# Embedding weights on ScalarE's DMA queue with the constants behind them, and a value bias that GpSimd sums for one product

## The reference, cut to what matters

```python
h = conv(x, conv_w) + conv_b + pos_table[pos_ids]       # 16x16 patches, no overlap
z = causal_attention(layernorm(h))                      # v = x W_V + b_V
h = h + einsum('bqhm,hmd->bqd', z, W_O) + b_O
h = h + moe(layernorm(h))                               # top 2 of 8 experts
```

## Time and profile before

| | |
|---|---|
| median of 3 runs | 194.37 us (193.43 to 194.73) |
| the profiled execution, whole time | 194.5 us |
| its span in the profile | 192.7 us |
| TensorE busy | 183.2 us, 95% of the span |
| VectorE, ScalarE, GpSimd busy | 123.9, 91.5, 65.3 us |
| TensorE's mean granted clock | 0.991 of full speed |

### The profile page before, as it was taken

One profiled execution on the slowest core, in us unless ns is written; L12 is line 12 of the kernel. 1 busy time (PEld: TensorE's weight loads), 2 busy tenths in 40 slices (PEclk: granted clock), 3 DMA queues, 4 the chain that ended last, 5 costly groups with the idle time before them and its releaser, 6 DMA issues.

```text
span 192.7 us, 4810 instructions
## 1 busy us (share of the span) xinstructions
PE 183.2 (95%) x1883; PEld 170.4 (88%) x1883; DVE 123.9 (64%) x371; ACT 91.5 (47%) x187; POOL 65.3 (34%) x99
## 2 busy tenths in 40 slices
PE   7999999999999999999999699999999999999991
PEld 2798999998898999998989586899999999999991
DVE  0257966876671065999897638788468467396283
ACT  2046530135455603466596445765857647553210
POOL 8632500114004000168568417550452514406000
PEclk9999999999999999999999969999999999999999
DMA  6999978007100000001108330115949579414544
GB/s 187 384 415 418 389 238 330 3 2 241 37 0 16 3 0 5 3 16 42 52 12 234 135 97 12 31 34 141 425 139 328 153 267 321 146 39 108 152 117 125
DMA packets 11642, 27.94 MB, mean 145 GB/s; under 512 B 3309, under 2 KB 6474, under 8 KB 10436
## 3 DMA queue, kind: packets, MB, share of 16 engines
q1 hardware_dynamic: 8868, 24.92, 38.0%
q0 software_dynamic: 2208, 2.21, 4.1%
q10 hardware_dynamic: 544, 0.50, 0.9%
HBM read 24.22 MB, written 5.77 MB: 156 GB/s over the span
## 4 chain that ended last, share of the span: by engine, by line
PE 70%; DMA 11%; DVE 8%; ACT 4%; issue 3%; POOL 1%; SPq 1%; POOLq 1%; DVEq 0%; ACTq 0%
PE ps L380 8%; PE ps L662 7%; PE ps L459 6%; PE ps L490 6%; DMA slots<-row,slot 3%; PE ps L625 3%; PE ps L647 3%; PE ps L644 3%; PE ps L626 3%; PE ps L648 3%; DMA kT<-parts 3%; PE ps L437 3%; DMA xp<-patches 3%; PE ps L466 2%; PE ps L440 2%
## 5 line engine op out<-in xcount | busy, mean ns | idle before, releaser
L1029 POOL DMA_INDIRECT parts<-qT,toke x12 | 17.9, 1490 | 30.6 <-ACT qT L903 28.8
L1265 DVE TENSOR_TENSOR wqkv<-raw,wqkv 128x1024 fp32r<-128x1024 f32 x16 | 19.6, 1222 | 4.1 <-ACT wqkv L826 3.4
L662 PE MATMUL ps<-xp,v 128*123 128x192 f32 x128 | 22.1, 326 | 0.0
L1354 DVE TENSOR_TENSOR v<-v,ps 128x246 f32<-128x246 f32 x32 | 12.4, 407 | 13.6 <-ACT v L891 13.6
L662 PEld LDWEIGHTS ps<-xp,v 128*123 128x123 f32 x128 | 20.6, 186 | 0.0
L490 PE MATMUL ps<-wo,zs 128*112 128x192 f32 x84 | 16.8, 349 | 1.9 <-ACT zs L792 1.9
L784 ACT ACTIVATE prob<-sm 128x588 f32<-128x588 f32 x8 | 5.7, 707 | 27.3 <-DVE sm L1088 27.3
L625 PE MATMUL ps<-zeA,wqkv 128*128 128x246 f32 x64 | 18.1, 291 | 0.3 <-ACT zeA L884 0.3
L997 POOL DMA_INDIRECT slots<-row,slot x14 | 14.7, 1052 | 9.8 <-DVE row L1180 3.4
L644 PE MATMUL ps<-zeA,wqkv 128*128 128x246 f32 x64 | 17.9, 279 | 0.0
L647 PE MATMUL ps<-zeR,wqkv 128*128 128x246 f32 x64 | 17.8, 278 | 0.0
(11 more groups left out here) (189 smaller groups left out, 475.9 us busy)
## 6 DMA issues: line engine op xcount, KB each, us to landing
raw<-w SPq DMA_DIRECT2D x8, 1024.0 KB, 6.8
xp<-w SPq DMA_DIRECT2D x8, 384.0 KB, 3.3
xp<-patches SPq DMA_DIRECT2D x8, 294.0 KB, 5.0
raw<-w_qkv SPq DMA_DIRECT2D x3, 768.0 KB, 6.0
slots<-blank SPq DMA_DIRECT2D x8, 196.0 KB, 4.4
xp<-slots SPq DMA_DIRECT2D x8, 196.0 KB, 4.4
parts<-zeros SPq DMA_DIRECT2D x1, 1176.0 KB, 8.7
convw<-conv_w SPq DMA_DIRECT2D x2, 288.0 KB, 4.4
```

The source lines that it names most:

```text
L662: last = mm(ps[0:EROWS, 6 + r, 0:D], hT[:, j, jt, r * EROWS:(r + 1) * EROWS], w2s[:, j, jt, :], start=(jt == 0), stop=(jt == JT - 1))
L1029: P.indirect_dma_start(parts, bass.IndirectOffsetOnAxis(toke[:, e, r:r + 1], 0), ye[0:EROWS, e % 2, r, :], None, bounds_check=TOPK * N + E ...
L1265: last = V.tensor_tensor(wsp[:, j, 1, half, :], raw13[j][:, half * W13:(half + 1) * W13], wsp[:, j, 0, half, :].bitcast(f32), ALU.subtract)
```

## The change

The first half of `convw` is no longer SP's first DMA but ScalarE's. ScalarE then waits until it has landed and only then issues the constants, `rowwise` now ahead of `columns`. The fillers of TensorE go from 10 to 8. GpSimd clears one more tile (`onesf`, 128x98, all ones) and, behind `norm` of pairs 0 to 5, sums `wo` times the value bias over the six chunks into `bvw` (128x192): one product, then five times a product and an addition. TensorE multiplies `onesf` by `bvw`, one fp32 matmul in the place of six. ScalarE's copy into `bvx` is gone.

```diff
-        bvx = sb("bvx", [128, HP, PT])
+        bvw = sb("bvw", [128, D])
+        bvc = sb("bvc", [128, D])
+        onesf = sb("onesf", [128, PT])
...
-            sp.dma_start(convw[:, 0:CA], conv_w[:, 0:CA]).then_inc(ld_conv[0], 16)
             sp.dma_start(xp[:, 0], patches[0]).then_inc(ld_x[0], 16)
...
-                pe.wait_ge(ld_wo, 16)
-                pe.wait_ge(bvx_ready, 1)
+                pe.wait_ge(bvw_ready, 1)
                 pe.wait_ge(h_ready, PH)
-                for c in range(HP):
-                    mm(ps[0:PT, 7, 0:D], bvx[:, c, :], wo[:, c, :], start=(c == 0), stop=(c == HP - 1))
+                mm(ps[0:PT, 7, 0:D], onesf[:], bvw[:], start=True, stop=True)
...
-            keep_busy(10, 0)
+            keep_busy(8, 0)
...
+            act.dma_start(convw[:, 0:CA], conv_w[:, 0:CA]).then_inc(ld_conv[0], 16)
+            act.wait_ge(ld_conv[0], 16)
+            act.dma_start(rowwise[:], by_row).then_inc(ld_rowwise, 16)
             act.dma_start(columns[:], by_column).then_inc(ld_columns, 16)
-            act.dma_start(rowwise[:], by_row).then_inc(ld_rowwise, 16)
...
-            A(bvx[:], bv[:, :, None].to_broadcast([128, HP, PT]), ACT.Copy).then_inc(bvx_ready, 1)
...
+            P.memset(onesf[:], 1.0)
             P.memset(seen[:], 0.0).then_inc(all_zeroed, 1)
...
+            def value_bias():
+                nonlocal n
+                pool.wait_ge(ld_wo, 16)
+                pool.wait_ge(ld_columns, 16)
+                P.tensor_scalar(bvw[:], wo[:, 0, :], bv[:, 0:1], 0.0, ALU.mult, ALU.add)
+                for c in range(1, HP):
+                    P.tensor_scalar(bvc[:], wo[:, c, :], bv[:, c:c + 1], 0.0, ALU.mult, ALU.add).then_inc(pool_seq, 1)
+                    n += 1
+                    pool.wait_ge(pool_seq, n)
+                    last = P.tensor_tensor(bvw[:], bvw[:], bvc[:], ALU.add)
+                    if c < HP - 1:
+                        last.then_inc(pool_seq, 1)
+                        n += 1
+                        pool.wait_ge(pool_seq, n)
+                last.then_inc(bvw_ready, 1)
...
             for p in range(EARLY):
                 norm(p)
+            value_bias()
```

More of the change, by code:

```diff
@@ L201, in vit_block @@
         h2T_ready, row_ready, bscale_ready = (sem(x) for x in ("h2T_ready", "row_ready", "bscale_ready"))
-        bvx_ready, bo_done, bo_ready = (sem(x) for x in ("bvx_ready", "bo_done", "bo_ready"))
+        bvw_ready, bo_done, bo_ready = (sem(x) for x in ("bvw_ready", "bo_done", "bo_ready"))
         both_ready, gap_ready, ratio_ready = (sem(x) for x in ("both_ready", "gap_ready", "ratio_ready"))
```

## The result

The changed kernel is slower: a median of 196.11 us (17 runs, 194.5 to 197.2 but for one disturbed execution) against 194.73 for the kernel before on the same chip, a ratio of 1.0089 with a 95% interval of 1.0056 to 1.0122. That is 1.1 to 2.4 us more. The forecast was 192.7 us, 1.7 us less. A second measurement on another chip gave 1.0054 (1.0016 to 1.0092).

What follows compares the result with a forecast made beforehand. The prediction took TensorE's busy time as the bound, with the queries' start set by VectorE's chain from embed(0). It summed 194.5 - 1.63 (bias) - 0 (start) = 192.87, less 0.13 for the median: 192.7 us, range 191.5 to 194.1.

Steps and rivals of the forecast that it cites:

- The product: Value bias on TensorE: five of six matmuls go, 1.63 us saved, all on the path; GpSimd's added work costs 0.
- rival (d): GpSimd's bias sum comes late, slowed beside VectorE, and TensorE waits; at 1.6 us an instruction 196.3 us; chance 0.04.
- upper bound of 7.3: GpSimd's six products and five additions for the bias: forecast 6.5 us, with bounds 4.9 to 7.3.
- The start: Up to the queries: conv(0) 1.3 us sooner, but `rowwise` lands at 8.05, embed(0) near 8.4, so net gain 0.
- My upper bound, 9.75: Latest landing of `rowwise`, from `convw` at 5.1 plus 4.6 us issue to landing; embed(0) at 10.1, a loss of 1.75.
- Rival (b): `rowwise` is slower, as in its old row: the start loses up to 1.75 us, giving 194.4; chance 0.09.
- 2.68 us of gain: Range's lower end: start gain of up to 1.05 us from a quicker `rowwise` (chance 0.32) plus the bias's 1.63.
- The first packet: ScalarE's issue of `rowwise`: 1.0 us to its first packet; the skill's 0.6 would land it 0.4 us sooner.
- rival (e): TensorE's idle time at the start, about 1.0 us near 16.4, lowers its clock, costing 1.0 us: 193.7; chance 0.07.

Runs made afterwards that it cites:

- the bias alone: Value bias summed on GpSimd, start as in the kernel before, run on two chips: 191.87 us, ratio 0.9865, and 192.96 us, ratio 0.9891, to the kernel before.
- The three runs with 2.3, 1.5 and 0.6 MB in front of it: Changed kernel, 196.11 us; with attention weights held until `xp` of pair 1 landed, 193.6 us; with SP's later transfers held until `convw`'s first half landed, 192.97 us.
- the start alone: Changed kernel with the value bias put back to six products and ScalarE's copy, queues and eight fillers as changed: 197.01 us, ratio 1.013 to the kernel before.

## Why the prediction was wrong

**What bounds the kernel, right.** The queries hang on VectorE's chain from embed(0): the distance from embed(0) to the queries was 10.8 us in both profiles and 10.8 to 11.1 in all experiments.

**The product, right.** 1.64 us of 1.63, all of it on the path up to 110 us, and 1.3% and 1.1% in the two ratios of the bias alone. GpSimd's products took 0.42 us (0.45 forecast), its additions 0.60 (0.59), and two products beside VectorE's L1271 of the old numbering took 0.76 and 1.11, as rival (d) expected. (That rival read its rows wrong in one point. The 1.14 us of the earlier trace rows are a two-input instruction, which takes 0.54 by itself in this trace, not 0.19.) The whole was 7.4 us (27.68 to 35.04) in place of 6.5, a little over the upper bound of 7.3, and still 6.6 us early.

**The start, wrong, and this is the step that failed:** "It then shares the 16 engines with `xp` of pairs 2 and 3 on SP's queue". I took the first packet at 1.0 us from the issue and half of the rate from there, 8.05 for the landing. It was 11.40. Of the 3.35 us between them 2.6 lie ahead of the first packets, which came at 8.2 and not 1.0 us behind the issue; 0.9 lie behind them, 3.2 us for moving and landing in place of 2.26, with `columns`, `earlier` and `masks` on the same queue; and the issue was 0.2 sooner than forecast. A share near half is what two queues got that were filled at the same time, as at the start of both kernels. `rowwise`, issued while the other queue had a backlog, got nearly nothing until 0.3 MB of that backlog were left, and 0.2 MB with the attention weights held back. The three runs with 2.3, 1.5 and 0.6 MB in front of it show this, and the run without the wait and the one with `rowwise` ahead of it show that on the same queue, but issued at 1.14, it lands at 6.9 and 6.6. No run issues it from SP. My upper bound, 9.75, was the old time from issue to landing, taken when only 0.4 MB had been issued ahead (`columns` and half of `convw`), and so was no bound. Rival (b) had the direction and half of the size. A slip beside it: by its own terms, 2.68 us of gain and 0.5 of spread, the lower end of the range is 191.2 and not 191.5.

**How the two queues shared.** In the first 3.9 us after, SP's queue moved 0.32 MB and ScalarE's 0.29; between 4.6 and 8.2 us it was 518 packets against 2. The Trainium skill's page "DMA: Bandwidth & Descriptors", section "Issuing engines are not separate DMA queues", says that DMAs of several engines run on the same 16 engines and interleave whoever issued them. The first pair of numbers agrees with it and the second doesn't: interleaving is what transfers issued together did here.

**The first packet.** With next to no backlog that of `rowwise` moved 1.3 us behind the start of its issue (4.48 to 5.8 us), somewhat over the 1.0 of my sum. At the start of the kernel before the first packets moved at 1.75 us, 1.0 behind the start of the first issue and 0.6 behind its end (0.73+0.40 = 1.13). The Trainium skill's page "DMA: Bandwidth & Descriptors", section Specifications, gives some 0.6 us for the first byte. Counted from the issue's end the trace agrees with it, so there was nothing to take off the measured 1.0 us, as I did in the prediction.

**The clock, rival (e), half right.** It fell behind TensorE's idle time at the start in the second profile of the changed kernel and in that of the start alone, but the idle time was 3.35 and 3.81 us, not 1.0, and of it VectorE's chain covered all but 0.2 us. The fall behind 110 us was there before the change, and between the two profiles it makes 1.5 us.

**The time.** By the profiles the change costs 1.82 us at 46.87 us; the ratios on two chips give 1.1 to 2.4 and 0.3 to 1.8 us. The measured loss may lie at the lower side because of the executions of the kernel before that start with slow passes. Such a start costs that kernel 2.4 us, for its embed(0) hangs on conv(0); the changed kernel's embed(0) hangs on `rowwise`, and in its profile, where the first four passes were slow too, TensorE was done with conv(0) nearly four us before `rowwise` landed. This is an argument from the profiles, and was not measured by itself.

## What to carry to other kernels

A wait in front of a DMA issue can cost more than its own length: here whatever the other queue had been given meanwhile went first, so divide that backlog by the measured rate before moving an issue back (1.7 MB at 0.38 MB/us is an estimate of 4.5 us; the first packets came after 3.6). Find the chain that sets the stage's end first; bringing one of its two inputs in sooner is worth nothing when the other one is made late. And judge parts of a change one by one: here one half won 1.6 us and hid behind the other's 3.5.

## What the runs showed that I had not expected

`rowwise` needed 6.8 us from issue to landing behind 1.7 MB of backlog, 5.2 behind 0.9 MB and 3.8 with next to none. The passes of an embedding behind 0.75 us without work took 527 ns in place of 326 at a granted clock of 1.00 in the rows, so that row alone doesn't tell how long a pass takes; the bias alone had an idle time of 0.80 us at the same place and 326 ns. What differed was that its fillers had gone from 634 to 379 ns before they ended, and those of the slow execution had not. And a queue's turn went by the time of the issue, on either queue: with the attention weights held back it was SP's queue that stood still, from 8.0 to 8.5 us.
